# Splitting all four chunks of both adjacency matrices, with GpSimd making two of the four low parts of each, and a new order of the first batches and the tail

## The reference

```python
h = jnp.maximum(_layernorm(x, axis=-1), 0.0)
A_fwd = [A1, A2, shifted]                      # A1 = A2 = adj, shifted = eye rolled by one row
A_list = A_fwd + [jnp.swapaxes(a, 1, 2) for a in A_fwd] + [eye]
HW = einsum('bnf,rfo->rbno', h, W[:, :F]) + einsum('rd,rdo->ro', W_edges, W[:, F:])[:, None, None, :]
out = x + jnp.max(einsum('rbnm,rbmo->rbno', A, HW), axis=0) + b
```

## Time and profile before

| | us |
|---|---|
| median of 3 runs | 217.32 (216.86 to 217.63) |
| the profiled execution | 216.98 |
| its span, first to last instruction | 215.3 |
| TensorE busy | 206.3 (96%) |
| VectorE busy | 177.0 (82%) |
| ScalarE busy | 160.8 (75%) |
| GpSimd busy | 95.9 (45%) |
| TensorE's granted clock, mean of the span | 0.989 of 2.4 GHz |

### The profile page before, as it was taken

One profiled execution on the slowest core, in us unless ns is written; L12 is line 12 of the kernel. 1 busy time (PEld: TensorE's weight loads), 2 busy tenths in 40 slices (PEclk: granted clock), 3 DMA queues, 4 the chain that ended last, 5 costly groups with the idle time before them and its releaser, 6 DMA issues.

```text
span 215.3 us, 3420 instructions
## 1 busy us (share of the span) xinstructions
PE 206.3 (96%) x902; PEld 149.5 (69%) x902; DVE 177.0 (82%) x414; ACT 160.8 (75%) x431; POOL 95.9 (45%) x140
## 2 busy tenths in 40 slices
PE   7799779999999999999999999999999999999994
PEld 7456456777767777777767777776777777777772
DVE  3574997988889797988989798888979798888755
ACT  3779788697896969698796969689696969876220
POOL 3112946446172735527082644617273552718200
PEclk9999979999999999999999999999999999999998
DMA  5999995376693939678492938769393938610101
GB/s 175 313 345 370 376 362 199 108 292 245 202 336 93 380 79 313 215 253 283 156 355 69 374 127 295 241 198 335 86 384 89 342 130 253 234 53 0 50 0 49
DMA packets 31587, 47.14 MB, mean 219 GB/s; under 512 B 1632, under 2 KB 11088, under 8 KB 31568
## 3 DMA queue, kind: packets, MB, share of 16 engines
q1 hardware_dynamic: 31568, 46.92, 64.3%
HBM read 42.72 MB, written 4.19 MB: 218 GB/s over the span
## 4 chain that ended last, share of the span: by engine, by line
PE 84%; SPq 6%; DMA 5%; DVE 2%; issue 1%; ACT 1%; POOL 0%; DVEq 0%; ACTq 0%; POOLq 0%
PE bank_p L761 11%; PE bank_p L763 10%; PE bank_p L762 9%; PE bank_g L725 6%; PE bank_gT L704 6%; PE bank_g L730 5%; PE bank_g L729 5%; PE bank_g L736 5%; DMA adj_sb<-in_adj_dram 5%; PE bank_gT L716 5%; PE bank_gT L710 5%; PE bank_gT L709 4%; PE bank_p L751 3%; PE bank_p L679 3%; PE bank_p L671 3%; PE bank_g L762 2%
## 5 line engine op out<-in xcount | busy, mean ns | idle before, releaser
L321 POOL TENSOR_TENSOR a_lo<-adj_sb,a_hi 128x512 fp32r<-128x512 f32 x15 | 19.4, 1295 | 72.3 <-DVE h_lo L548 68.5
L579 DVE TENSOR_TENSOR best<-bank_p,best 128x512 f32<-128x512 f32 x48 | 33.2, 691 | 8.4 <-PE bank_p L763 7.3
L434 ACT ACTIVATE gT_hi<-bank_gT 128x512 fp32r<-128x512 f32 x16 | 9.6, 598 | 30.9 <-PE bank_gT L716 30.5
L576 DVE SCALAR_TENSOR_TENSOR best<-bank_p,c_col,best 128x512 f32<-128x512 f32 x32 | 24.0, 750 | 5.8 <-ACT best L453 5.1
L389 ACT ACTIVATE a_hi<-adj_sb 128x512 fp32r<-128x512 f32 x45 | 27.7, 620 | 1.3 <-DMA adj_sb<-in_adj_dram 1.3
L402 ACT ACTIVATE aT_hi<-adjT_sb 128x512 fp32r<-128x512 f32 x45 | 27.7, 620 | 0.0
L315 POOL TENSOR_TENSOR o_sb<-best,x_bias 128x512 f32<-128x512 f32 x15 | 20.0, 1332 | 15.8 <-DVE best L579 15.8
L418 ACT ACTIVATE h<-x_sb,shift,rstd 128x128 f32<-128x128 f32 x60 | 24.7, 497 | 1.4 <-DVE shift L528 1.4
L542 DVE TENSOR_TENSOR aT_lo<-adjT_sb,aT_hi 128x512 fp32r<-128x512 f32 x30 | 24.5, 854 | 0.0
L729 PE MATMUL bank_g<-aT_hi,h_hi 128*128 128x512 f32 x45 | 24.4, 541 | 0.0
L709 PE MATMUL bank_gT<-a_hi,h_hi 128*128 128x512 f32 x45 | 23.6, 525 | 0.0
(11 more groups left out here) (110 smaller groups left out, 501.8 us busy)
## 6 DMA issues: line engine op xcount, KB each, us to landing
adj_sb<-in_adj_dram SPq DMA_DIRECT2D x15, 1024.0 KB, 5.6
adjT_sb<-in_adjT_dram SPq DMA_DIRECT2D x15, 1024.0 KB, 5.6
xT_sb<-in_xT_dram SPq DMA_DIRECT2D x16, 256.0 KB, 5.9
x_sb<-in_x_dram SPq DMA_DIRECT2D x15, 256.0 KB, 6.1
out_dram<-o_sb SPq DMA_DIRECT2D x15, 256.0 KB, 5.9
adj_sb<-in_adj_dram SPq DMA_DIRECT2D x4, 256.0 KB, 3.4
adjT_sb<-in_adjT_dram SPq DMA_DIRECT2D x4, 256.0 KB, 4.8
w_sb<-in_W_dram SPq DMA_DIRECT2D x3, 128.0 KB, 4.5
```

Of the source, the lines that this page charges most:

```text
L579: op = nc.vector.tensor_tensor(best[q][:, :], product, best[q][:, :], ALU.max)
```

## The change

All four chunks of both directions are split from batch 1 on. `WHOLE` and `SPLIT` go. `ND = 2` chunks have their low part made by VectorE and `NG = 2` by GpSimd:

```diff
-WHOLE = (0,)
-SPLIT = (1, 2, 3)
-NS = len(SPLIT)
-ND = NS - 1
+ND = 2
+NG = 2
+NS = ND + NG
-WARM_UP = 10
+WARM_UP = 7
...
             def split_adj_last(b):
-                pool.wait_ge(ahi_ready, b * NS)
-                nc.gpsimd.tensor_tensor(a_lo[q][:, ND, :], adj_sb[q][:, C - 1, :], ...
+                for c in range(ND, NS):
+                    pool.wait_ge(ahi_ready, (b - 1) * NS + c + 1)
+                    nc.gpsimd.tensor_tensor(a_lo[q][:, c, :], adj_sb[q][:, c, :], ...
...
-                nc.scalar.activation(h_hi[q][:, :, :], h[q][:, SPLIT[0]:, :], ACT.Copy)
+                nc.scalar.activation(h_hi[q][:, :, :], h[q][:, :, :], ACT.Copy)
...
             def aggregate_T(b):
-                for c in WHOLE:
-                    nc.tensor.matmul(bank_gT[:, 0:N], h[q][:, c, :], adj_sb[q][:, c, :], ...
+                for c in range(C):
+                    pe.wait_ge(ahi_ready, (b - 1) * NS + c + 1)
+                    nc.tensor.matmul(bank_gT[:, 0:N], h_hi[q][:, c, :], a_hi[q][:, c, :], ...
...
             add_bias(0)
+            part_sums(1)
             split_adjT_last(1)
             add_bias(1)
             for b in range(1, B):
-                part_sums(b)
                 finish(b - 1)
                 if b + 1 < B:
                     pool.wait_ge(hlo_ready, b + 1)
                     split_adj_last(b + 1)
                     add_bias(b + 1)
+                    part_sums(b + 1)
                     split_adjT_last(b + 1)
...
             load_x(2)
+            load_adj(2)
             sp.dma_start(bias_sb[:, :], biasT).then_inc(bias_in, 16)
             load_xT(0)
+            load_adjT(2)
             load_xT(1)
+            load_x(3)
```

More of the change, by code:

```diff
@@ L400, in split_adjT @@
                     act.wait_ge(g_psum, b - 1)
[L401 to L405, removed]
+                for c in range(C):
+                    last = nc.scalar.activation(aT_hi[q][:, c, :], adjT_sb[q][:, c, :], ACT.Copy,
                                                 accum_out=sums[q][:, 1, c:c + 1])
-                last.then_inc(sums_ready, 1)
+                    last.then_inc(aThi_ready, 1)
             def make_h(b):
@@ L454, in begin_best @@
                                      bias=c_col[:, ORDER[0]:ORDER[0] + 1]).then_inc(best_begun, 1)
+            for i in range(2):
+                half = slice(i * HALF, (i + 1) * HALF)
+                act.dma_start(x_sb[0][:, half, :], x_dram[0][:, half, :]).then_inc(x0_in[i], 16)
             act.wait_ge(ident_ready, 1)
@@ L518, in variance, with first_variance, first_scale_and_shift @@
                 last.then_inc(aggr_done, 1)
+            def first_variance(i, stats_sem, aggr_sem):
+                dve.wait_ge(x0_in[i], 16)
+                for c in range(i * HALF, (i + 1) * HALF):
+                    last = nc.vector.bn_stats(stats[:, c, :], x_sb[0][:, c, :])
+                last.then_inc(stats_sem, 1)
+                dve.wait_ge(stats_sem, 1)
+                nc.vector.memset(wait_carrier[:, :], 0.0)
+                for c in range(i * HALF, (i + 1) * HALF):
+                    last = nc.vector.bn_aggr(mean_var[0][:, c, :], stats[:, c, :])
+                last.then_inc(aggr_sem, 1)
+            def first_scale_and_shift(i, std_sem, rstd_sem, shift_sem):
+                half = slice(i * HALF, (i + 1) * HALF)
+                dve.wait_ge(std_sem, 1)
+                nc.vector.reciprocal(rstd[:, half], std[:, half]).then_inc(rstd_sem, 1)
+                dve.wait_ge(rstd_sem, 1)
+                nc.vector.scalar_tensor_tensor(out=shift[:, half], in0=mean_var[0][:, half, 0], scalar=-1.0,
+                                               in1=rstd[:, half], op0=ALU.mult, op1=ALU.mult).then_inc(shift_sem, 1)
             def scale_and_shift(b):
                 dve.wait_ge(std_ready, b + 1)
-                if b >= 1:
-                    dve.wait_ge(h_ready, b)
+                dve.wait_ge(h_ready, b)
                 if b == 1:
@@ L628, in _ @@
             split_h_lo(1)
+            split_adj_lo(1)
             variance(2)
-            take_best(0, 2)
-            split_adj_lo(1)
-            for i in range(NH, NPROD):
+            for i in range(2, NPROD):
                 take_best(0, i)
```

195 lines of the change are left out of this document (103 added, 92 removed).

## The result

The changed kernel takes 229.34 us (median of 4 runs, 227.98 to 229.71), the one before 217.47 in the same comparison. The ratio is 1.054 [1.050, 1.058]: slower by 5.4%, where 4.7% was forecast. The profiled execution took 229.71 us, its span 228.0.

A forecast was written before the change was run, and what follows sets the result against it. TensorE bounds the kernel before; after the change a 12.83 us ring through VectorE and GpSimd sets the pace. 42.3 + 0.5 + 166.8 + 16.7 - 0.5 = 225.8 us span, plus 1.7: 227.5 us, range 220 to 232.5.

The forecast's parts named there:

- TensorE's saving: Middle batches: three fp32r passes replace one whole chunk, saving 0.14 to 0.15 us a direction; TensorE alone needs 12.0 a batch.
- The turns at the port: Shared SBUF port: a GpSimd turn holds VectorE back 1.18 us, a VectorE turn holds GpSimd about 0.52.
- The ring: Middle: hand-overs between VectorE and GpSimd from shift to shift sum to 12.83 us a batch and set the pace; chance 0.70.
- the case that the prediction gave 12.98: Middle: VectorE asks only after finish has begun, so both its aT_lo come behind it, 3.71 us in place of 3.56.
- A rule that the turns count whole: Port: each turn counts in full, 1.30 and 0.68 us, making the ring 0.4 longer, 232 to 233 us in all; chance 0.06.
- TensorE waits 0.8 us: Middle: in each batch TensorE waits 0.8 us for hT_lo, ahead of the first product with hT.
- The rival with the clock falling in every batch: Middle: waiting lowers TensorE's clock in each batch, 13 x 0.9 us more, 235 to 240 us; chance 0.05.
- Two of its signs for the middle: Trace of the middle: VectorE's aT_lo pair about 2.9 us, not 1.5; GpSimd idle ahead of a_lo far less than 4.95.
- The start: Batch 1: bias behind adj(2) holds GpSimd's a_lo to 23.6 us, shift ends at 34.2, batch 2 begins 3.5 later, at 42.3.
- TensorE reaches batch 1 sooner: Start: TensorE comes to batch 1 earlier, but without gain, since the bias holds batch 1 up.
- The clock: Batch 1: a fall of TensorE's clock into the products costs 0 to 1.7 us more; 0.5 taken.
- The tail: Last batch and end: 0.3 us saved by the passes, 0.2 (0 to 0.5) by two half-width edge terms; 16.7 becomes 16.2.

The follow-up runs named there:

- GpSimd lightened: Changed kernel, but from batch 3 on GpSimd leaves out the low part of chunk 2 in both directions; 218.34 us, ratio 1.005.
- the three experiments on the middle: Changed kernel with GpSimd's output sum late, 218.34 us; with one low part less on GpSimd, 218.34 us; previous kernel with GpSimd's two subtractions made twice, 226.56 us.
- the kernel with the old start and the late sum: Previous kernel's loads and first batches, with all chunks split, new tail, GpSimd's output sum late and x_bias of batch 1 behind o_sb; 214.41 us, ratio 0.986.
- the kernel with the repairs on the new start: Changed kernel with GpSimd's output sum late, ten warm-ups, bias and first xT ahead of adj(2), x_bias of batch 1 behind o_sb; 214.89 us, ratio 0.990.

## Why the prediction was right

It said 227.5 us and slower; 229.34 was measured. The mechanism of the middle was right, and it carries most of the loss, 7.6 of the 12.7 us between the two spans. The start came out near by errors that partly cancel. Step by step:

- **TensorE's saving** (0.14 to 0.15 a direction): 0.17 in direction T, and 12.05 a batch with GpSimd lightened, where 12.0 was said. Right.
- **The turns at the port** (1.18 and 0.52 us): in the batch shown first, pair and o_sb measure 2.35 and 1.82; the terms give 0.52 + 1.18 + 0.68 = 2.38 and 0.52 + 1.30 = 1.82. Right, and the three experiments on the middle show that it is this meeting that costs.
- **The ring**, 12.83 a batch: 12.87 measured on average. The ten even batches are 12.89 to 12.95; the average is pulled by batches 2 (12.01, with o_sb nearly over when VectorE asks), 3 (13.28) and 14 (12.77). The eight with o_sb first are the case that the prediction gave 12.98, both of VectorE's behind finish. By its terms, in the batch shown first: shift's end to a_lo 129.22 - 126.06 = 3.16 (3.17). What it did not see is a second ring beside GpSimd's: hT_lo, TensorE's products, VectorE's maxima, the pair stretched by 0.84, and hT_lo again. By the rows the two are within 0.1 us of each other, since VectorE asks for the pair at T + 2.15, as the earlier trace rows had it, and finds GpSimd within 0.06 of the end of its own. Which of the two sets the pace, no run tells. A rule that the turns count whole, which the prediction took from the Trainium skill's "SBUF — State Buffer", section "SBUF: two separate sides", would have made it 0.4 longer; the batches of 12.89 to 12.95 don't agree with that. The trace does agree that the loser stands still meanwhile: VectorE's first takes 1.79 us behind o_sb, where one alone takes 0.68.
- **TensorE waits 0.8 us** for hT_lo: 0.69 in the batch shown, and by the page's waits 11.7 us in 13, of which 2.6 in batch 1: 0.76 on average in the others. Right. The rival with the clock falling in every batch is refuted: the windows read 1.00 from 45 us on.
- **Two of its signs for the middle** did not come. VectorE's pair was to take about 2.9 us and takes 2.35 to 2.40. The prediction's own wait of 0.8 and margin of 0.1 ask for 1.51 + 0.9 = 2.4, so the 2.9 did not fit its own sum. GpSimd was to be idle ahead of a_lo for far less than 4.95 us and is idle for 3.99 to 4.59; the prediction's 12.83 less 8.4 of work left 4.4.
- **The start.** The links of the chain were right in their order, and its end nearly so: the shift's end was to be at 34.2, and it is at 33.87. Luck has a part in that. What released its first link was not the bias (23.6 said) but ScalarE's a_hi, at 22.91, late because batch 0's passes were slow, which the prediction did not foresee; and the a_lo pair took 3.02 and not 2.5, since it met VectorE's own a_lo. The bias had landed at 22.06. The megabyte ahead of it took 2.7 us, as reckoned (x(2) landed at 18.67, adj(2) at 21.38), but all before it landed 1.4 us sooner than in the kernel before (x(2) at 20.07 there). SP's list begins with adj now, issued at 0.80 and not at 1.80, since x(0) had left it, and the prediction left that out. With batch 0 on time, in the run with ten warm-ups, the shift ends at 32.87, 1.3 us before the 34.2.
- **"TensorE reaches batch 1 sooner"** is wrong for the profiled execution: 23.15 after 21.54, since batch 0's first passes took 5.9 us. Where they took their usual time it is right, 20.84 to 21.03. "I count them at nothing", said of the other edits at the start, was then wrong by 1.0 us, within the "up to 1 us" that it allowed.
- **The clock**, 0.5 with 1.7 as the bound: 8.65 - 6.38 = 2.3. This is the term that was mis-sized. It is 1.8 of the 2.2 us by which the profiled execution lies over 227.5. The bound was taken from the fall in the kernel before, a full-speed loss of 1.7 us. The windows after hold 0.47 + 0.50 of 3.5 us each, 3.4 us of loss: twice that. The stretch at half clock lasted 3.4 us before the change and 6.8 in the changed kernel, and 6.8 in each of the six other runs that have one. One observed fall is no upper bound on the next.
- **The tail**, 16.2: 16.4. The passes gave their 0.3. The two edge terms, put at 0.2, gave nothing: the kernel with the new tail and the old split takes 16.69 from the start of batch 15, and 16.68 before.

42.8 + 166.8 + 16.2 + 1.7 was said, and 44.25 + 167.4 + 16.4 + 1.7 measured.

## What to carry to other kernels

An idle engine is not a free one: before giving it work, look at what it will stand next to on a port, and at whether its last instructions still end before the bottleneck's partner asks. The order within the helper's turn can matter more than its load: here one wait on GpSimd was worth 11 us of 229. A margin of a few tenths between the busiest engine and its supplier is not seen in the busy shares; it has to be read from two timelines side by side.

## What the runs showed that was not expected

- Eight 128x512 passes of float32 took 5.3 to 5.9 us in four of the five profiled kernels with seven warm-ups, and 3.6 to 3.9 in all five with ten. The row of granted clocks reads 1.00 for these windows, but the traces' first clock record stands at 9.56 to 10.83 us in the four slow ones and at 4.78 to 7.72 in the other six, and in each the time over 3.6 is, within 0.1 us, half of the stretch by which the passes began ahead of that record, or nothing where they began behind it. So it is TensorE's lower clock at the start of the program, which the row does not show. One with seven was normal (3.7), so the number of warm-ups doesn't decide it alone; that seven make the late rise more frequent than ten is likely, but not shown.
- A fall of the clock in batch 1 costs between nothing and 2.7 us of the way from hT_lo to batch 2, by what is running when it comes. It follows a stretch in which TensorE waits, but not every such stretch is followed by one: in the kernel with the old start and the late sum TensorE was busy for only 1.73 of the 3.5 us from 31 on, and no fall shows in the profiled execution. Its median lies 0.5 us under that of the kernel with the repairs on the new start, with intervals that overlap.
- A small instruction can wait as long as a large one: shift, 128x4, took 1.04 us beside o_sb of GpSimd.
